# VectorE's setup split in three parts and laid into the first graph's preparation

## The reference

```
# layer 0
adj1 = adj + I;  s = degree(adj1)**-0.5
x = layernorm(x + s * adj1 * s @ (x @ w0) + b0)
# layer 1
m_j = x @ W1[:D];  m_i = x @ W1[D:]
msg[i,j] = gelu(layernorm(m_j[j] + m_i[i] + b1) * g1 + be1)      # D = 128 values per pair
agg[i] = sum_j adj[i,j] * msg[i,j]
upd = layernorm(concat(x, agg) @ W2 + b2) * g2 + be2
out = layernorm(x + upd)
```

## Time and profile before

| | us |
|---|---|
| Median of 3 timed runs | 3895.66 |
| Lowest, highest | 3895.11, 3899.29 |
| Span of the profiled execution, first to last instruction | 3892.5 |
| TensorE busy | 3535.2 (91%) |
| VectorE busy | 3188.3 (82%) |
| ScalarE busy | 3278.9 (84%) |
| GpSimd busy | 1785.5 (46%) |

### The profile page before, as it was taken

How to read it: one execution, slowest core, us unless ns; L and a number is a source line. 1 busy time by engine, 2 the same in 40 slices (tenths; PEclk the granted TensorE clock), 3 DMA queues, 4 the chain that set the end, 5 groups by cost and what they waited for, 6 DMA issues and landing times.

```text
span 3892.5 us, 92785 instructions
## 1 busy us (share of the span) xinstructions
PE 3535.2 (91%) x29118; PEld 3242.9 (83%) x29119; DVE 3188.3 (82%) x7469; ACT 3278.9 (84%) x8841; POOL 1785.5 (46%) x1206
## 2 busy tenths in 40 slices
PE   3699999999989989999999999999999999999997
PEld 2588888888878888888888888888888888889887
DVE  3588888889878888888888878888888888888987
ACT  2688898889869889887988888888898989888987
POOL 2454554445533455443555344554444555434531
PEclk9899999999989999999999999999999999999999
DMA  1222211222211222122221122221122221122210
GB/s 38 84 83 87 80 63 55 74 85 88 79 52 48 86 78 85 45 66 80 88 79 62 45 80 88 79 88 56 56 78 86 88 79 64 57 69 86 75 65 16
DMA packets 305520, 276.43 MB, mean 71 GB/s; under 512 B 16688, under 2 KB 263984, under 8 KB 304944
## 3 DMA queue, kind: packets, MB, share of 16 engines
q1 hardware_dynamic: 272176, 168.59, 14.3%
q0 software_dynamic: 32768, 100.70, 7.0%
HBM read 160.17 MB, written 109.05 MB: 69 GB/s over the span
## 4 chain that ended last, share of the span: by engine, by line
PE 66%; ACT 12%; DVE 11%; issue 8%; POOL 1%; ACTq 1%; DVEq 0%; DMA 0%; SPq 0%; POOLq 0%; PEldq 0%
PE agg_even_ps L1268 11%; PE z_even_ps L1306 11%; PE z_odd_ps L1306 11%; PE agg_odd_ps L1268 10%; ACT tmp L657 4%; PE p_ps L1122 3%; PE z_even_ps L1302 3%; PE z_odd_ps L1302 3%; DVE pick L1028 2%; ACT msg L642 2%; ACT root L594 2%; DVE spread L1060 2%; PE t_ps L1207 2%; PE p_ps L1109 1%; PE t_ps L1201 1%
## 5 line engine op out<-in xcount | busy, mean ns | idle before, releaser
L657 ACT ACTIVATE tmp<-nbr,r_sb 128x128 f32<-128x128 f32 x4608 | 1445.3, 390 | 29.2
L462 POOL DMA_INDIRECT table<-stage,row_id x512 | 802.3, 1567 | 410.2 <-issue 399.3
L1028 DVE SCALAR_TENSOR_TENSOR pick<-rank,root_p 128x512 f32<-128x512 bf16 (+3 forms) x1664 | 932.1, 587 | 42.4 <-ACT rank L613 42.3
L1060 DVE SCALAR_TENSOR_TENSOR spread<-rankT,nbr 128x512 f32<-128x512 bf16 (+3 forms) x1664 | 867.4, 548 | 0.0
L642 ACT ACTIVATE msg<-msg 128x768 f32<-128x768 f32 (+1 forms) x896 | 728.8, 813 | 36.3 <-issue 33.0
L1268 PE MATMUL agg_odd_ps<-spread,msg 128*128 128x128 f32 x5120 | 662.5, 280 | 62.4 <-ACT msg L642 36.2
L1268 PEld LDWEIGHTS agg_odd_ps<-spread,msg 128*128 128x128 f32 x5120 | 622.3, 196 | 70.7 <-ACT msg L642 42.1
L1306 PEld LDWEIGHTS z_even_ps<-mi_g,pick 128*128 128x128 f32 x5120 | 643.1, 196 | 30.8 <-issue 1.7
L1306 PE MATMUL z_even_ps<-mi_g,pick 128*128 128x129 f32 x5120 | 663.7, 280 | 0.0
L1306 PEld LDWEIGHTS z_odd_ps<-mi_g,pick 128*128 128x128 f32 x5120 | 626.7, 192 | 30.2 <-issue 0.5
L1306 PE MATMUL z_odd_ps<-mi_g,pick 128*128 128x129 f32 x5120 | 647.1, 276 | 0.0
(11 more groups left out here) (222 smaller groups left out, 5008.0 us busy)
## 6 DMA issues: line engine op xcount, KB each, us to landing
nbr<-table SPq DMA_DIRECT2D x256, 256.0 KB, 4.0
adj_g<-in_adj SPq DMA_DIRECT2D x32, 1024.0 KB, 6.1
nbr_root<-table SPq DMA_DIRECT2D x128, 256.0 KB, 3.2
nbr_heavy<-table SPq DMA_DIRECT2D x128, 128.0 KB
x_g<-in_x SPq DMA_DIRECT2D x32, 256.0 KB, 3.4
table<-stage,row_id POOLq DMA_INDIRECT x512, 4.3
out<-out_sb SPq DMA_DIRECT2D x32, 256.0 KB, 2.3
w_sb<-in_L_gnn_W SPq DMA_DIRECT2D x2, 128.0 KB, 2.4
```

The source lines that it names most:

```text
L462: pool.indirect_dma_start(table[q], bass.IndirectOffsetOnAxis(ap=row_id[:, jt * TB + it:jt * TB + it + 1], axis=0), stage[:, jt, it, :], N ...
L657: last = act.activation(tmp[:, c % 2, n - FROM[u], :], half_row, ACT.Identity, scale=r_sb[:, c % 2, n - FROM[u]:n - FROM[u] + 1])
L1028: ins = dve.scalar_tensor_tensor(into.rearrange("p k n -> p (k n)"), rank[:, it, span], float(MARK + t), root_p[:, it, span], ALU.is_equal ...
L1060: ins = dve.scalar_tensor_tensor(into, rankT[:, it, jt:jt + count, :], float(MARK + t), nbr[:, it, jt:jt + count, 0:P], ALU.is_equal, ALU. ...
```

## The change

The setup becomes three functions, and they are called from VectorE's `alone()` ahead of step 3 (weights), step 8 (small constant tiles) and step 12 (splits). be1 is split once and copied to the two other blocks. The adding of `MARK` to `lower` (was L756) goes with the weights. TensorE and ScalarE start without the setup; TensorE waits for `s_const` ahead of its first use of w0, for `s_setup` 1 ahead of its first use of W1, and for `s_setup` 2 ahead of m_j of graph 0. GpSimd's order of the first steps of graph 0 changes from 0, 1, 2, 3, 4, 5 to 0, 1, 3, 4, 2, 5: its power (L402) is now issued before the 0/1 matrix (L428). For all other graphs nothing changes.

```
 # GpSimd, alone()
-                for s in range(GC):
+                for s in (0, 1, S_X, S_X + 1, S_EDGE) + tuple(range(S_SUP, GC)):
                     root_of_x(0, s)
                     prepare(0, 0, s)
                     scatter(0, 0, s)
 # ScalarE
-            act.wait_ge(s_setup, 1)
+            act.wait_ge(s_ident, N_IDENT)
 # VectorE
-            dve.wait_ge(s_const, 16 * N_CONST)
             dve.wait_ge(s_ident, N_IDENT)
             step(dve.memset(x_v[:, :], 1.0))
+            def setup_weights():
+                dve.wait_ge(s_const, 16 * N_CONST)
...
+                step(dve.scalar_tensor_tensor(lower[:, :], ident[:, :], float(MARK), lower[:, :], ALU.mult, ALU.add))
+                dve.sem_inc(s_setup, 1)
+            def setup_limits():
...
+            def setup_splits():
+                for rows in (mi_split[:, :], b2_split[:, :], be_split[:, :, :]):
+                    step(dve.memset(rows, 0.0))
+                split(mi_split[0:3, :], b1_all)
+                split(b2_split[0:3, :], b2_all)
+                split(be_split[0:3, 0, 0:D], be1_all)
+                step(dve.tensor_copy(be_split[0:3, 1:3, :], be_split[0:3, 0:1, :].to_broadcast([3, 2, D + 1])))
+                dve.sem_inc(s_setup, 1)
             def alone():
                 for s in range(GC):
+                    if s == S_X:
+                        setup_weights()
+                    if s == S_PRE:
+                        setup_limits()
+                    if s == S_HT:
+                        setup_splits()
                     for slot in range(RUNS):
                         last_run(0, None, 0, s, slot)
                         prepare(0, 0, s, slot)
 # TensorE
-            pe.wait_ge(s_setup, 1)
                 if s == S_SUP:
                     free(F_SUP)
+                    if is_int(a, 1):
+                        pe.wait_ge(s_const, 16 * N_CONST)
                 if s == S_MIT:
+                    if is_int(a, 1):
+                        pe.wait_ge(s_setup, 1)
                 if s in (S_MI, S_MJ):
                     free(F_MI if s == S_MI else F_MJ)
+                    if is_int(a, 1) and s == S_MJ:
+                        pe.wait_ge(s_setup, 2)
```

More of the change, by code:

```diff
@@ L720, in split @@
                     step(dve.scalar_tensor_tensor(into, parts[0:3, k, :], ident[0:3, k:k + 1], into, ALU.mult, ALU.add))
-            dve.wait_ge(s_const, 16 * N_CONST)
             dve.wait_ge(s_ident, N_IDENT)
[L724 to L745, removed]
-            step(dve.memset(x_v[:, :], 1.0))
@@ L748, in _ @@
[L748 to L762, removed]
+            step(dve.memset(x_v[:, :], 1.0))
@@ new lines, in setup_weights @@
+            def setup_weights():
+                dve.wait_ge(s_const, 16 * N_CONST)
+                for k in range(2):
+                    step(dve.reduce_sum(mean1[:, k:k + 1], w1_sb[:, k, :], AX.X))
+                step(dve.reduce_sum(mean1[:, 2:3], b1_all, AX.X))
+                step(dve.tensor_scalar(mean1[:, :], mean1[:, :], -1.0 / D, None, ALU.mult))
+                for k in range(2):
+                    step(dve.tensor_scalar(w1_sb[:, k, :], w1_sb[:, k, :], mean1[:, k:k + 1], None, ALU.add))
+                    step(dve.tensor_tensor(w1g_sb[:, k, :], w1_sb[:, k, :], g1_all, ALU.mult))
+                step(dve.tensor_scalar(b1_all, b1_all, mean1[:, 2:3], None, ALU.add))
+                step(dve.tensor_scalar(b1_col[:, :], b1_col[:, :], mean1[:, 2:3], None, ALU.add))
+                for k in range(2):
+                    step(dve.scalar_tensor_tensor(w1_sb[:, k, 0:D - 1], w1_sb[:, k, D - 1:D].to_broadcast([P, D - 1]), TURN, w1_sb[:, k, 0:D - 1],
+                                                  ALU.mult, ALU.add))
+                    step(dve.memset(w1_sb[:, k, D - 1:D], 0.0))
+                step(dve.scalar_tensor_tensor(b1_col[:, :], b1_all[:, D - 1:D], TURN, b1_col[:, :], ALU.mult, ALU.add))
+                step(dve.scalar_tensor_tensor(b1_col[:, :], ident[:, D - 1:D], 0.0, b1_col[:, :], ALU.is_equal, ALU.mult))
+                step(dve.tensor_tensor(b1_all, b1_all, g1_all, ALU.mult))
+                step(dve.scalar_tensor_tensor(lower[:, :], ident[:, :], float(MARK), lower[:, :], ALU.mult, ALU.add))
+                dve.sem_inc(s_setup, 1)
@@ new lines, in setup_limits @@
+            def setup_limits():
+                for k in range(TB):
+                    step(dve.memset(first_slotT[:, k:k + 1], float(MARK + CAPS[k] + 1)))
+                    step(dve.memset(first_slot[:, k + 1:k + 2], float(MARK + CAPS[k] + 1)))
+                for into in (first_slotT[0:HEAVY_W, 0:1], first_slot[:, 0:1]):
+                    step(dve.memset(into, float(MARK + CAPS[0] + HEAVY_TILES * HEAVY_T + 1)))
+                step(dve.tensor_copy(ident_b[:, :], ident[:, :]))
+                for k, limit in enumerate(LIMITS):
+                    step(dve.memset(limits[:, k:k + 1], float(limit)))
+                for k in range(HEAVY_T):
+                    for m in range(HEAVY_TILES):
+                        step(dve.memset(behind_p[k * HEAVY_W:(k + 1) * HEAVY_W, m:m + 1], -float(m * HEAVY_T + k)))
+                step(dve.tensor_copy(o_slot[:, :], first_slot[:, :]))
+                step(dve.tensor_copy(o_slotT[:, :], first_slotT[:, :]))
```

## The result

| | before, us | after, us |
|---|---|---|
| Median of the timed runs (4 and 4) | 3895.39 | 3870.77 |
| Lowest to highest | 3891.26 to 3899.29 | 3867.20 to 3872.30 |
| Span of the profiled execution | 3892.5 | 3869.9 |

The ratio of the runs is 0.9931, with a 95% interval of 0.9917 to 0.9946; the medians differ by 24.6 us, or 0.6%. The change is faster, clear of the noise. The forecast was 3869.0 in 3863 to 3876. The spans of the two profiled executions differ by 22.6 us, for 26.7 forecast. The profiled execution of the changed kernel took 3871.74 us, 1.84 more than its span.

What follows compares the result with a forecast made beforehand. TensorE was taken to bound the loop, VectorE's setup the opening. The start's 23.3 us and the new order's 3.35 gave 26.7 off the 3892.5 span, 3865.8; with 3.2 from span to median, 3869.0, range 3863 to 3876.

Steps and rivals of the forecast that it cites:

- Start: TensorE no longer waits for VectorE's setup, only for graph 0's loads: first matmul at 17.2 for 40.51, 23.3 us earlier.
- New order: GpSimd's power ahead of the 0/1 matrix in graph 0: 3.35 us more gain at L796, beyond the start's.
- Rival B: The new order gives nothing: L796 at 36.5 to 38.6, gain 23.3 to 25.4 us; 13 in 100.
- Meeting: TensorE's adjacency product and GpSimd's self term both release VectorE's L796, at about 35.3 for 61.97, 26.7 us earlier.
- GpSimd's side: GpSimd's path to L796: L428 from 24.75 to 32.4, then L419 and L422 from 32.6 to 35.2.
- Small constants: VectorE's constant tiles before step 8: 4.5 us, from 25.0 to 29.5, slack 5.8, hidden by L428 and L1122.
- Splits: VectorE's block before step 12: 10.4 us, ending at 52.7; m_j at 58.4 leaves slack 5.7, cost nothing.
- Rival C: Gain partly given back further on, by splits, placing or second graph's GpSimd chain; half lost gives 3882; 7 in 100.
- The first indirect DMA: GpSimd's first indirect DMA, which needs the row numbers, at 67.5 for 94.19, 26.7 us earlier.
- Loads: Graph 1's load, waiting for the end of L428, at 32.4 for 53.1; wanted 35 us later, so hidden.
- The clock's spread: Graph 0's work falls at other moments of TensorE's clock changes: 3 us either side for the whole opening.
- Rival D: Slower: the loop, entered at another moment, gets more half-level stretches; 40 more would give 3919; 3 in 100.

Runs made afterwards that it cites:

- e2: The changed kernel with GpSimd's old order of graph 0's steps, so the earlier start alone; median 3874.22 us, ratio to before 0.9947.
- e1: The changed kernel run again unaltered; median 3868.17 us, ratio to before 0.9941.
- e3: The kernel before with only GpSimd's new order of graph 0's steps; median 3891.22 us, ratio to before 0.9994 (interval 0.9985 to 1.0003).
- e12: The changed kernel unaltered, a third time, on another chip; median 3869.18 us, ratio to before 0.9936.
- e4: The changed kernel with the whole block of splits ahead of step 12 done twice; median 3871.50 us, ratio to before 0.9948.
- e5: The changed kernel with graph 0's 0/1 matrix made by VectorE in place of GpSimd's L428; median 3866.36 us, ratio to before 0.9934.
- e7: The changed kernel with 50 TensorE products ahead of the loads and graph 0's 0/1 matrix on VectorE; median 3865.22 us, ratio to before 0.9932.
- e11: The changed kernel with TensorE kept busy through graph 0's steps and into graph 1's, 0/1 matrix on VectorE; median 3858.59 us, ratio to before 0.9913.
- e8: The changed kernel with TensorE kept busy up to the adjacency product, L428 still on GpSimd; slow chip, median 4041.76 us, ratio to before 0.9928.
- e9: The filling of e8 with graph 0's 0/1 matrix on VectorE; slow chip, median 4035.44 us, ratio to before 0.9924.
- e6: The changed kernel with 50 TensorE products into an unused bank ahead of the loads; median 3866.41 us, ratio to before 0.9942.

## Why the prediction was right, point by point

- *Start*: forecast 17.2, measured 16.83, released by the load; 23.7 us for 23.3. Right (also e2).
- *Weights before step 3*: end forecast at 19.4, measured 19.1, with 2.5 us of slack for 2.6. Right.
- *New order*: 3.35 forecast, 3.4 from e2 and e1 and from e3 and before, at equal products. Right. Rival B (the order gives nothing) is ruled out.
- *Meeting*: forecast 35.3, measured 35.91. Both sides were placed right (GpSimd 35.2 forecast, 34.04 measured; TensorE 35.2 and 35.76). The term that was mis-sized is TensorE's product with the adjacency, taken at its old 5.66: it took 6.66 in this execution. In five executions of the change's own order it was 5.19, 5.94, 6.66, 6.76 and 6.78 (e1, e12, after, e4, e5), so a single number was the wrong form for it. The bound of 6.9 held. The statement that TensorE "keeps about its 5.66" has no ground in the runs; nothing ties the rise of the clock to the work in front of it that closely.
- *GpSimd's side* ended 1.2 us earlier than forecast: 0.4 is the earlier load, 0.4 an instruction of VectorE between degree and power, which took 0.61 beside L428 before and takes 0.17 now, and 0.3 the issue ahead of L419, which I had added and which doesn't show.
- *Small constants*: 4.5 us forecast, 24.47 to 29.0 measured. Right, and the copies beside L428 were not held (0.17 each for the two small ones, 0.23 for the cast). The one that was held is L792, which the prediction had priced at nothing. It had taken from L779 that the trace shows no hold beside L428; but the trace of before also has L778 just ahead of it, 0.61 at the start of L428 for 0.17 in the change.
- *Splits*: 10.4 forecast, 42.88 to 53.12 measured, 10.2; the copy that had no row took 0.22 for 0.3. The slack of 5.7 is 5.9 to 6.1 by e4 and by the rows. Rival C's place is the right one, and the block isn't long enough for it.
- *The first indirect DMA*: forecast 67.5, measured 68.32, the 0.6 of the meeting and 0.2 of clock; the loop starts 25.1 earlier, and graph 1's product with the adjacency lost 0.4 of it.
- *Loads*: graph 1's is issued at 31.6, forecast 32.4. It stays hidden: graph 1's first transpose, at 69.86, waits for ScalarE.
- *The clock's spread*: 3 us on either side. From the first matmul to the loop start the three executions of the change took 93.98, 91.21 and 92.49. Right.
- *Luck*: the span came out at 3869.9 for 3865.8, 4.1 off, and the median only 1.8 off. The sum added 3.16 from span to median, and this time the median lies 0.87 above the span of the profiled execution, which was the second slowest of the four. So an error of 4.1 and one of 2.3 went against each other. The prediction had also named it a sign of being wrong if the first indirect DMA comes earlier and the span doesn't: 25.9 against 22.6. Of these 3.3, 0.8 lie between the indirect DMA and the loop start (0.4 in graph 1's product with the adjacency, 0.3 in L1320, 0.81 for 0.49) and 2.5 in the loop, 1.3 of them in its first product, 2.79 for 1.50. The like product took 2.70 to 2.79 in e2, e3 and e7 too, and 1.50 in e1 and e12, which are the change itself: this comes and goes from one execution to the next.
- *A slip in rival C*: half of the gain is 13.3 us, 0.34%, and not under 0.2%. Nothing in the forecast rests on it.
- *The whole*: 26.7 forecast, 24.6, 24.5 and 24.0 measured by medians in three sets of runs. The openings of the profiled executions of the change gained 25.1, 28.1 and 27.8 over the one of before; in e3, on e1's chip, the constants landed 1.7 earlier than in that one, so part of the 28.1 may be its late constants. On that chip e1 starts its loop 24.1 earlier than e3, and the medians are 23.0 apart. The loops are 3759.1, 3757.7 and 3759.3 for 3756.6. Over all runs on chips of like speed they are 3755.1 to 3760.9, with no order by how early they start: e4 has the shortest and e11, 16 us earlier, one of the longest. The mean of those that start early is 3758.8 (nine), of before and e3 3756.1 (two). So a give-back of some 2 us in the loop is neither shown nor excluded, and of the executions of before there is one profile. This stays open. Rival D (the loop pays some 27 us or more) is ruled out.

## What to carry to other kernels

A wait at the head of a queue for a whole setup costs all of the setup that the first users don't need: give each user its own wait, and lay the blocks into the gaps of the engine that makes them. Where two engines meet, write down both ends: taking 7.6 us off one side gave 3.4, and removing L428 from GpSimd altogether gave nothing until TensorE's side had been shortened too (e5, e8, e9). In an opening of many short waits TensorE runs at half level, and filling its gaps, with L428 taken off GpSimd as well, was worth 10 us more (e11 beside e12). Filling that stopped at the meeting started the loop no earlier in its one profile (e8).

## What the runs showed of the hardware that I had not expected

- The granted clock reads 1.00 in the opening of each run until it first falls, also where TensorE is slow. The stretch of the change's product with the adjacency (columns as in the earlier trace rows):

```profile
29.10:35.80 6.70, 6.66 (x32) 6.46 (x32) 0.00 (x0) 0.00 (x0) 4.67 (x4) 1.00 0.41 129
```

  The same 32 records take 3.84 us where TensorE had been kept busy. The column doesn't show the half level at the start of a kernel; the durations do. The Trainium skill (TensorE: Matmul & The Clock Gate, What's actually happening) calls the lower level the default, and the runs agree with it and not with the column.
- Busy ahead of the loads isn't enough: with 50 products before them the fourth group of transposes (e6, at 21.32) was slow again, and the granted clock from 20 to 28 us reads 0.59. With 3 more products in each gap the product with the adjacency took 3.84 each time (e8 to e11).
- A VectorE instruction that reads two tensors and starts beside GpSimd's L412 ended with L412: in e3, where the constants came earlier, it was L738 that took 1.25 beside L412, and L737 took 0.16, the other way round than in the earlier trace rows. In e8 it was the adding to `lower`, with 128 columns, 1.24 for 0.29. Beside L428 the holds were shorter and came only at its start, 0.59 for 0.16 at L792.
